# Stacking query and key rows for the attention: sixteen SBUF-to-SBUF transfers a tensor in place of a round trip through internal memory

## The reference

```python
q = (query @ Wq + bq).reshape(B, Nq, H, D).transpose(0, 2, 1, 3)      # H = 16, D = 16
k = (key_value @ Wk + bk).reshape(B, Nkv, H, D).transpose(0, 2, 1, 3)
v = (key_value @ Wv + bv).reshape(B, Nkv, H, D).transpose(0, 2, 1, 3)
attn = jnp.einsum('bhqd,bhkd->bhqk', q, k) * scale
attn = jnp.clip(attn, -CLAMP, CLAMP)
attn = jax.nn.softmax(attn, axis=-1)
```

## Time and profile before

| | us |
|---|---|
| median of 3 runs | 1577.71 |
| runs | 1579.04, 1563.91, 1577.71 |
| the profiled execution | 1566.94 |
| its span, first to last instruction | 1564.9 |
| mean granted clock of TensorE | 0.933 of full speed |

### The profile page before, as it was taken

How to read it: one execution, slowest core, us unless ns; L and a number is a source line. 1 busy time by engine, 2 the same in 40 slices (tenths; PEclk the granted TensorE clock), 3 DMA queues, 4 the chain that set the end, 5 groups by cost and what they waited for, 6 DMA issues and landing times.

```text
span 1564.9 us, 23343 instructions
## 1 busy us (share of the span) xinstructions
PE 1326.4 (85%) x9071; PEld 1118.8 (71%) x9071; DVE 1075.8 (69%) x1729; ACT 570.1 (36%) x1171; POOL 800.9 (51%) x762
## 2 busy tenths in 40 slices
PE   6996999999989989977798989896582798989890
PEld 6985788778868868855566766665452798989890
DVE  4655766766676676543777677677673688888886
ACT  3666211211111021123344444443330565666552
POOL 4343666656656566523222433534443776767652
PEclk9997999999999999999999999998685899999995
DMA  5100333233223233212233215323400855555525
GB/s 167 37 21 1 111 94 115 81 92 98 81 81 99 76 94 94 61 39 56 94 99 120 82 40 120 88 58 95 115 8 25 293 211 192 209 191 207 192 71 161
DMA packets 58044, 163.23 MB, mean 104 GB/s; under 512 B 10598, under 2 KB 26185, under 8 KB 50000
## 3 DMA queue, kind: packets, MB, share of 16 engines
q1 hardware_dynamic: 45760, 100.13, 22.2%
q0 software_dynamic: 12176, 61.63, 11.1%
HBM read 136.47 MB, written 27.08 MB: 105 GB/s over the span
## 4 chain that ended last, share of the span: by engine, by line
PE 60%; DVE 17%; issue 7%; DMA 6%; ACT 5%; SPq 3%; POOL 2%; ACTq 0%; POOLq 0%; DVEq 0%
PE bank L388 13%; PE bank L390 13%; PE bank L389 13%; PE bank L1210 9%; PE bank L396 4%; SPq L717 3%; DVE topE L1714 2%; DVE hid_hi L1589 2%; DMA split_qk<-qk_lo 2%; PE bank L1052 2%; DVE shiftE L1723 2%; DMA xt_hi<-split_qk 2%; DVE hf L1605 2%; PE bank L1039 1%; PE bank L1128 1%
## 5 line engine op out<-in xcount | busy, mean ns | idle before, releaser
L520 POOL TENSOR_TENSOR wpiece_lo<-wraw,wpiece_hi 128x1024 fp32r<-128x1024 f32 x88 | 216.9, 2464 | 7.4
L1591 DVE TENSOR_TENSOR hid_lo<-hf,hid_hi 128x512 fp32r<-128x512 f32 x96 | 213.8, 2227 | 3.3
L388 PE MATMUL bank<-hid_hi,wpiece_lo 128*128 128x512 f32 x512 | 202.4, 395 | 12.9 <-DVE hid_lo L1591 12.9
L390 PE MATMUL bank<-hid_hi,wpiece_hi 128*128 128x512 f32 x512 | 200.7, 392 | 0.0
L389 PE MATMUL bank<-hid_lo,wpiece_hi 128*128 128x512 f32 x512 | 200.7, 392 | 0.0
L518 POOL TENSOR_SCALAR wpiece_hi<-wraw 128x1024 fp32r<-128x1024 f32 x88 | 95.0, 1080 | 186.2 <-PE bank L390 182.3
L1589 DVE CAST hid_hi<-hf 128x512 fp32r<-128x512 f32 x96 | 79.6, 830 | 125.7 <-ACT hf L1326 124.6
L1326 ACT ACTIVATE hf<-bank,ffn_scales 128x512 f32<-128x512 f32 x64 | 44.2, 690 | 293.8 <-PE bank L390 293.8
L636 POOL TENSOR_SCALAR staging<-staging 128x1024 f32<-128x1024 f32 x64 | 66.7, 1041 | 138.9 <-ACT staging L1411 138.6
L1210 PE MATMUL bank<-w_hi,gh_lo 128*128 128x256 f32 x368 | 106.1, 288 | 22.5 <-issue 21.8
L388 PEld LDWEIGHTS bank<-hid_hi,wpiece_lo 128*128 128x128 f32 x512 | 96.8, 189 | 39.1 <-DVE hid_lo L1591 19.3
(11 more groups left out here) (337 smaller groups left out, 3711.4 us busy)
## 6 DMA issues: line engine op xcount, KB each, us to landing
wraw<-in_C_w SPq DMA_DIRECT2D x88, 512.0 KB, 3.6
split_qk<-qk_hi SPq DMA_DIRECT2D x64, 128.0 KB, 2.4
split_qk<-qk_lo SPq DMA_DIRECT2D x64, 128.0 KB, 2.4
xt_lo<-split_qk SPq DMA_DIRECT2D x8, 1024.0 KB, 5.5
xt_hi<-split_qk SPq DMA_DIRECT2D x8, 1024.0 KB, 6.9
yc<-y_rows SPq DMA_DIRECT2D x16, 256.0 KB, 6.2
ctx_raw<-in_ctxT SPq DMA_DIRECT2D x16, 192.0 KB, 3.7
xraw<-in_xT SPq DMA_DIRECT2D x8, 256.0 KB, 3.5
```

What stands on the lines that cost most here:

```text
L388: pe.e.matmul(o, sl, mh, start=start and i == 0, stop=False)
L390: made = pe.e.matmul(o, sh, mh, start=False, stop=stop and i == n - 1)
L520: pool.e.tensor_tensor(pair[1], raw, f(pair[0]), ALU.subtract).then_inc(done, 1)
L1591: dve.e.tensor_tensor(lo[:, o, :], hf[o % 2][:, :], f(hi[:, o, :]), ALU.subtract).then_inc(s_hid, 1)
```

## The change

In `stack_heads` the copy through the internal tensor `split_qk` goes: 8 transfers a tensor of 64 partitions (128 KB each) into it and one of 1 MB out of it. In their place 16 transfers a tensor, each of 32 partitions and 2 KB a partition (64 KB), go from `qk_hi` or `qk_lo` to every fourth partition of the stacked operand: one for each copy r and each group j of pairs. The wait for the last scores of sequence b - 2, which frees the operand's buffer, stands in front of the first transfer instead of in front of the 1 MB load. `stored` counts 16 transfers for 8, and TensorE waits for the two semaphores of the rows, as the semaphore of the 1 MB loads no longer exists. Both before and after, 1 MB a tensor arrives in the operand.

```diff
-        split_qk = ring(2, lambda i: nc.dram_tensor(f"split_qk{i}", (2, 2, 4, 4 * DH, KC * S), F32, kind="Internal").ap())
...
-                line.wait_ge(w_qk[which], 16 * 8 * ((n + 1 - which) // 2))
+                line.wait_ge(w_qk[which], 16 * 16 * ((n + 1 - which) // 2))
...
-                n, held = 2 * b + which, split_qk[b % 2][which]
-                sp.wait_ge(l_qk[b % 2], 16 * 2 * (b // 2))
+                n, held = 2 * b + which, (q_e if which else k_e)[b % 2]
+                if b >= 2:
+                    old = use["E", "s", b - 2, PAIRS - 1]
+                    sp.wait_ge(old.filled, old.full)
                 for part, (src, done) in enumerate(((qk_hi, s_qkhi), (qk_lo, s_qklo))):
                     sp.wait_ge(done, n + 1)
                     for r in range(4):
                         if (r // 2 if which else r % 2) == part:
-                            for i in range(2):
-                                load(held[i, r], f(src[i * 4 * DH:(i + 1) * 4 * DH, :, :]).rearrange("p c s -> p (c s)"), w_qk[which])
-                sp.wait_ge(w_qk[which], 16 * 8 * (b + 1))
-                if b >= 2:
-                    old = use["E", "s", b - 2, PAIRS - 1]
-                    sp.wait_ge(old.filled, old.full)
-                load(f((q_e if which else k_e)[b % 2]).rearrange("p j s -> p (j s)"),
-                     held.rearrange("i r (d j) s -> (i r d) (j s)", j=4), l_qk[b % 2])
+                            for j in range(4):
+                                load(f(held[r::4, j * KC:(j + 1) * KC, :]), f(src[j::4, :, :]), w_qk[which])
...
-                    pe.wait_ge(l_qk[b % 2], 16 * 2 * (b // 2 + 1))
+                    for which in range(2):
+                        pe.wait_ge(w_qk[which], 16 * 16 * (b + 1))
```

More of the change, by code:

```diff
@@ L350, in build @@
         s_vone, s_prob = sem("ones"), sem("e_prob")
-        s_qkhi, s_qklo, w_qk, l_qk = sem("e_qkhi"), sem("e_qklo"), ring(2, lambda i: sem(f"w_qk{i}")), ring(2, lambda i: sem(f"l_qk{i}"))
+        s_qkhi, s_qklo, w_qk = sem("e_qkhi"), sem("e_qklo"), ring(2, lambda i: sem(f"w_qk{i}"))
         s_rm, s_re, s_rf, s_rb, s_rs, s_sh = (sem(f"r_{n}") for n in ("m", "e", "f", "b", "s", "sh"))
```

## The result

The median of six runs is 1607.79 us (1601.8 to 1624.12), against 1575.7 us for the kernel before (six runs, 1563.91 to 1579.04): a ratio of 1.0244, 95% interval 1.0202 to 1.0286. The change makes the kernel 2.4% slower; 1605 was predicted. The ratio is taken from all the runs; the two medians lie 32.1 us apart, a ratio of 1.020. The profiled execution took 1609.51 us with a span of 1607.4, 42.5 us longer than that of before. The profile of before was one of its shorter executions, 8.8 us under its median, so the two traces stand somewhat further apart than the typical executions do.

The account below looks back on a forecast made before the run. The run was taken as bound by TensorE, with in-order engines holding each other up in stage DE. The terms 26.7 - 5 + 10 + 3.3 gave +35 us, hence 1602 or 1613 by base; 1605 was predicted, range 1570 to 1640.

Parts of the forecast that it names:

- The k side: SP's issues of k rows: 16 at 0.64 us land 5.1 us later, stalling TensorE 26.7 us over sequences 0 to 5.
- about 10: Sign of being right: ScalarE's wait for the k rows at about 10 us in the first six sequences.
- There is no reserve: TensorE needs ScalarE's qk_raw almost at once, so the 5.1 us of later k rows go through.
- What comes back: VectorE works ahead while TensorE stands, so TensorE's waits for shiftE mostly go: 1.0 us in five sequences, -5.
- What the clock adds: New TensorE stalls in sequences 1 to 5 bring half clock behind them: 2.0 us each, +10.
- The q side: q operand in sequences 6 and 7, held by GpSimd's shifted scatters: +0.9 and +2.4 us, +3.3.
- completions seem to be held until some 13 us after the first of four scatters: DMA beside GpSimd's scatters, even writes into SBUF: q operand released at 1081.0 us in sequence 6, 1133.1 in 7.
- Cheap issue: Rival: new transfers issue near 0.37 to 0.5 us, mostly no change that can be told, 1567 to 1590; chance 0.19.
- No hold on SBUF: Rival: issue at 0.64 us but q's rows land freely, +24 us, 1591 to 1601; chance 0.11.
- Faster: Rival: cheap issue and no hold together, waits for the q operand vanish, -17 us, 1550 to 1561; chance 0.10.
- Small transfers cost more than their issue: Rival: 1.0 us per 64 KB transfer, k rows +10.9 instead of +5.1 in six sequences, 1640 to 1660; chance 0.05.
- In order, behind ScalarE's wait: ScalarE is in order: behind its wait for k rows stand qk_raw, the D projections' evictions, exponentials and features.

Follow-up runs that it names:

- experiment 9: Changed kernel with four unused matmuls added in TensorE's stall in sequences 1 to 5 and GpSimd's scatters four rounds later: 1613.68 us, ratio 1.0203.
- experiment 1: Changed kernel with a second set of qk_hi and qk_lo, so ScalarE needn't wait for the k rows to leave: 1578.27 us, ratio 1.0035.
- 5: Changed kernel with GpSimd's four scatters moved to a step of their own four rounds later: 1593.54 us, ratio 1.0256.
- experiment 6: Changed kernel with a second set of qk_hi and qk_lo and GpSimd's scatters four rounds later: 1548.77 us, ratio 0.9975.
- experiment 8: Changed kernel with four unused matmuls added for TensorE at its stall in sequences 1 to 5: 1590.74 us, ratio 1.0269.
- experiment 3: Changed kernel with eight direct transfers a tensor of 64 partitions instead of sixteen, rows in the wrong order: 1554.01 us, ratio 0.9894.
- experiment 2: Kernel before the change with a second set of qk_hi and qk_lo: 1578.12 us, ratio 1.0045.
- experiment 10: Changed kernel with twenty-four transfers a tensor, every second one of the sixteen cut into two: 1689.91 us, ratio 1.0671.

## Why the prediction was right, and where it wasn't

The direction, the time and the mechanism came out: 1605 against 1607.79, and a stage 37.5 us longer against a sum of +35. That they came out so closely is in part luck. The terms are less good than their sum, for two of them erred in opposite ways; and 1605 was set between two bases 11 us apart, while the difference itself is 32 us by the medians and 42.5 by the traces.

**The k side, pitch 0.64 us, 5.1 us later in each sequence.** Right. Starts of eight issues lie 5.0 to 5.5 us apart in sequences 5 to 7, and ScalarE's wait grew by 4.3 us from eight direct transfers to sixteen and by 5.0 to twenty-four. It came to 8.2 to 9.2 us where "about 10" was named, since landing took 1.9 us and not 2.4. The stalls in sequences 0 to 5 were put at 26.7 us; TensorE's waits there grew by 4.3 + 17.8 = 22.1, least in sequence 2 (2.5 us, where 3.4 was taken). "There is no reserve" held: the chain goes from the last landing through ScalarE to TensorE with gaps under 0.1 us.

**What comes back, -5.** The waits for `shiftE` fell by 3.7 us.

**What the clock adds, +10.** Its price came out and its size did not. The step took 5 us at half clock from the earlier trace rows for each of five sequences; the windows after show none in sequence 2, some 4 us in 1 and 3, and 12 us in 4 and 5. TensorE's busy time grew by 26.8 us instead of 10. By experiment 9 only some 10 of such an excess reach the stage, so +10 may be near what the clock is worth there, but by luck: the prediction equated busy time with stage time.

**The q side, +3.3.** This is the term that was mis-sized, with the sign wrong. From the first q issue to the use of the operand the kernel before needed 22.0 and 21.4 us in sequences 6 and 7; the changed one needs 1108.65 to 1125.25 and 1158.96 to 1175.78, 16.6 and 16.8 us (TensorE's timeline):

```profile
1125.25 0.50 PE L1103 MATMUL bank<-xt_lo,xt_hi 64*128 64x256 f32 x4 [2.31 <-issue]
...
1175.78 0.80 PE L1103 MATMUL bank<-xt_lo,xt_hi 64*128 64x256 f32 x4 [5.21 <-issue]
```

So 5 us were won on this path, which the later k rows took back. In waits, the operand's fell by 15.6 us and those for `qk_raw` in 6 and 7 rose by 7.3: -8.3 in place of +3.3. The step that failed is "completions seem to be held until some 13 us after the first of four scatters". The scatters did shift, to 1114.33 and 1164.64, but the operand was used 10.9 and 11.1 us after the first, and in sequence 3 of experiment 1 18.1 us after. What the prediction had read as a fixed delay from two events of before is none. Its own rows for sequence 6 didn't fit either: the q rows issued at 1062.47 landed 8.95 us later, at 1071.42, which is 8.5 us after the first scatter and not 13. That there is a hold is shown: in experiment 1 the operand is used 10.6, 10.7 and 9.2 us after the last issue in three sequences beside scatters and 1.4 us in one without, and these waits are gone in 5 and 6 when the scatters move. In sequences 6 and 7 of experiment 1, also beside scatters, it is 3.5 and 1.7 us. The Trainium skill ("DMA: Bandwidth & Descriptors", section "Queues, rings and completion order") has the increment of a transfer land behind the earlier writes of the same DMA engine on any queue; the 14.47 us landing of experiment 8 agrees, with SBUF as the source and the destination. No figure for its length stands there, and what sets it stays open.

By terms, 22.1 - 3.7 - 8.3 + 26.8 = +36.9, against 37.5 measured in DE. The forecast of 26.7 - 5 + 3.3 + 10 was 4.6 too high on the stalls and 11.6 on the q side, and 16.8 too low on the clock.

**The rivals.** *Cheap issue* fell with the 594 ns. *No hold on SBUF* fell with experiment 1, yet its result for sequences 6 and 7 was nearer than the forecast's. *Faster* needed both and had neither; but experiment 3 (0.9894) shows its reason sound: the round trip was on the path and worth 15.7 us, and the price of removing it was eight more issues. *Small transfers cost more than their issue* fell with the pitch: 0.64 us for 64 KB. The page of the Trainium skill that the prediction names, section "Bandwidth", has 0.95 us for 64 KB. That figure is the time of one transfer from HBM to SBUF over 128 partitions, issued from GpSimd, so it isn't a pitch of issues on SP's queue, and no run here measures it.

**"In order, behind ScalarE's wait"** was right, and the wait is the largest lever: a second buffer took back 29 us of 37.5. What the prediction didn't see is how closely the next things follow. Freed of the wait, the changed kernel meets the operand (40.5 us), the one before its load (34.5 us), and one kept at full clock the hold (17.8 us). None of these repairs gave its wait's worth alone.

Open are the share of the clock in the loss, since the ratios of 5, 8 and 9 overlap, why stalls of like length lower it for 4 us or for 12, and the length of the hold. Whether a layout exists in which eight transfers deliver the right rows was not tried, and neither was the moved wait for the old scores by itself; no row shows SP held by it.

## What to carry to other kernels

Count issues before bytes: on one queue each transfer of this kind costs its 0.6 us in series, whether it carries 32, 64 or 128 KB, so a copy that is split further pays for itself only if nobody waits for the last piece while it is being issued. Before a stage is charged for a stall, look at what TensorE does behind it, at what clock and for how long, and keep extra busy time and extra stage time apart. And where several waits in one loop are of like length, removing one shows the next; remove them together, or expect less than the wait was long (38.5 us of TensorE's waits went in experiment 1 and DE fell by 29.4; in experiment 2 nothing came of it).

## What the runs showed of the hardware

- An issue on SP's queue takes 594 to 598 ns in the median for 128, 64 and 32 KB over 64 or 32 partitions, while issues over 128 partitions took 328 ns (`wraw`, 512 KB) in the same program. In these rows the cost doesn't follow bytes.
- Landing followed size more than place: 128 KB took 2.4 us to internal memory and 2.3 to SBUF, 64 KB 1.9, 32 KB 1.8 (experiment 10).
- After stalls of 3.5 and 4.2 us (sequences 4 and 5) the granted clock stood at 0.50 and 0.52 for 12 us, although TensorE worked 11.5 and 10.3 of these; after 3.8 and 4.1 us (1 and 3) it was low for some 4 us, after 2.5 us (2) not at all. With four added matmuls (experiment 8) it was at 1.00 behind all five.
- Beside scatters on GpSimd's queue, SBUF-to-SBUF transfers on SP's completed up to 14.5 us after issue (experiment 8); with the scatters moved away they were used 1.4 us after the last issue (experiment 6). From the first scatter to the use it was 10.9 to 18.9 us.
